# Macaron block on eight cores: the requantised hidden rows scaled in a loop of their own, ahead of the transposes

## The chip, the cores and the metric

One Trainium2 chip, 8 cores. Each core runs the same program on one of the eight batch rows of the input (4096 tokens of 1024 features), with its own copy of the weights, and no core talks to another. The metric is the device time in microseconds (us) of the slowest core.

## The reference, cut to what matters

```
x = x + 0.5 * ffn(layernorm(x))
x = x + attn(layernorm(x))
x = x + 0.5 * ffn(layernorm(x))

def ffn(x, w_gate, w_up, w_down):        # 1024 -> 4096 -> 1024
    gate = silu(bitlinear(x, w_gate))
    up   = bitlinear(x, w_up)
    return bitlinear(gate * up, w_down)
def bitlinear(x, w):                     # ternary weights, 8-bit activations
    return act_quant(x) @ weight_quant(w).T
def act_quant(x):
    scale = 127.0 / clip(max(abs(x), over the row), 1e-5)
    return clip(round(x * scale), -128, 127) / scale
```

The attention is a gated linear recurrence (four 1024x1024 products and cumulative sums over the tokens) and isn't touched by the change. What matters here is the third `bitlinear` of `ffn`: its input `gate * up` has 4096 columns a token, its scale needs the maximum over all 4096 of them, and only then can it be rounded and multiplied.

## The kernel before, in words

The program has no scheduler: every engine's instructions stand in the order in which the Python code emits them, and every dependence is a wait on one of four counting semaphores, `cT` (TensorE), `cS` (ScalarE), `cV` (VectorE), `cG` (GpSimd), or on a DMA's.

A core works through 8 chunks of 512 tokens (`NCH`), each as 4 token tiles of 128 (`TT`, index `tt`). A chunk is FFN, attention, FFN, so `emit_ffn_rest` stands 16 times in the program. The weights are turned into ternary bf16 tiles once, at the start, written to scratch in HBM (`sc_g`, `sc_u`, `sc_d`) and loaded again in every FFN.

`emit_ffn_rest` has three stages:

1. Gate and up (lines 545 to 579): 512 matmuls of 128x512. ScalarE's `Silu` (L530) and VectorE's product (L533) put the float32 hidden values into `hbuf[:, tt, :]`, and L539 takes the partial maxima.
2. Requantise and transpose (lines 585 to 610), called the block below. For each `tt`: VectorE makes the scale in five tiny operations (L586, L589, L593, L594, L599); ScalarE scales and rounds the 4096 columns in place in one activation (L602: `x * s2v + MAGIC`); TensorE transposes them, 32 pieces of 128x128 in float32, and the results go as bf16 to `hq`. The transposes are emitted by `transpose_quads` (line 373), which takes four groups ("quads") of eight pieces. Quad 0 to 3 use PSUM columns 0, 1024, 2048 and 3072, that is all eight banks. Quads 0 and 2 are evacuated by VectorE (L394), quads 1 and 3 by ScalarE (L402). TensorE's first wait in each quad is for the counts `savedV` and `savedS`, which are the numbers of VectorE and ScalarE operations emitted so far when `transpose_quads` was called.
3. Down (lines 613 to 648): 16 loads of `sc_d` (L621, issued by ScalarE's queue, two ahead, the first two once all transposes are done) and 256 matmuls (L640) into all eight banks.

Between 2 and 3, in the second FFN of a chunk except the last, `pre_next` does the layer norm, quantisation (L479) and transposes of the next chunk's input. VectorE begins it with L327.

So in the block ScalarE's queue reads: scale tile 0, evacuate two quads, scale tile 1, evacuate two quads, and so on. L602 of tile `tt+1` stands behind the evacuation of quad 3 of tile `tt`, and all transposes of `tt+1` wait for it.

Of the kernel before, what the change touches and what calls it, by code (L numbers as in the profile page):

```python
# [39 lines left out]
def build_nc(L=4096, T=512):  # L40
    NCH = L // T
    TT = T // 128
# [108 lines left out]
    cV = Sem(st, nc, "cV")  # L151
    cS = Sem(st, nc, "cS")
# [3 lines left out]
    V, S, TE, SY, G = nc.vector, nc.scalar, nc.tensor, nc.sync, nc.gpsimd  # L156
# [213 lines left out]
        cV.inc(V.tensor_scalar(out=Bq, in0=Bq, scalar1=-1.0, scalar2=MAGIC,  # L370
                               op0=ALU.mult, op1=ALU.add))

    def transpose_quads(quads, evac="copy", eng="alt"):
        savedV = [cV.n] * 4
        savedS = [cS.n] * 4
        for qi, (srcs, dst) in enumerate(quads):
            b = qi % 4
            TE.wait_ge(cV.h, savedV[b])
            TE.wait_ge(cS.h, savedS[b])
            for j, s_ in enumerate(srcs[:-1]):  # L380
                TE.transpose(out=PB[:, b * 1024 + j * 128:  # L381
                                    b * 1024 + (j + 1) * 128],
                             in_=s_, identity=ident[:, :])
            cT.inc(TE.transpose(  # L384
                out=PB[:, b * 1024 + (len(srcs) - 1) * 128:
                       b * 1024 + len(srcs) * 128],
                in_=srcs[-1], identity=ident[:, :]))
            pt = PB[:, b * 1024:b * 1024 + len(srcs) * 128]
            if eng == "V" or (eng == "alt" and qi % 2 == 0):
                cT.wait(V)  # L390
                if evac == "copy":
                    cV.inc(V.tensor_copy(out=dst, in_=pt))
                else:
                    cV.inc(V.tensor_scalar(out=dst, in0=pt, scalar1=MAGIC,  # L394
                                           scalar2=None, op0=ALU.subtract))
                savedV[b] = cV.n
            else:
                cT.wait(S)
                if evac == "copy":
                    cS.inc(S.copy(out=dst, in_=pt))  # L400
                else:
                    cS.inc(S.add(out=dst, in_=pt, add=nmagic_ap))  # L402
                savedS[b] = cS.n
# [34 lines left out]
    def emit_ffn_pre(c, xb, first_of_chunk, p, skip01=False):  # L438
# [39 lines left out]
        for tt in range(TT):  # L478
# [3 lines left out]
        cS.inc(sl_)  # L482
        cS.wait(TE)
        transpose_quads(
            [([qstage[:, tt * 1024 + ic * 128:tt * 1024 + (ic + 1) * 128]
               for ic in range(DC)],
              aq[:, tt, :, :]) for tt in range(TT)], evac="submagic")

    def emit_ffn_rest(c, xb, p, pre_next=None, attn_next=None):
# [91 lines left out]
        if c == 0:  # L581
            for s_, n_ in tern_done["d"]:
                s_.wait(V, n_)
                s_.wait(S, n_)
        for tt in range(TT):
            cV.inc(V.reduce_max(out=hmax[:, tt:tt + 1],  # L586
                                in_=hpart[:, tt * 8:tt * 8 + 8], axis=AXX))
            cV.wait(V)
            cV.inc(V.tensor_scalar(out=hmax[:, tt:tt + 1],  # L589
                                   in0=hmax[:, tt:tt + 1], scalar1=EPS_Q,  # L590
                                   scalar2=None, op0=ALU.max))
            cV.wait(V)
            V.reciprocal(out=t1[:, tt:tt + 1], in_=hmax[:, tt:tt + 1])  # L593
            cV.inc(V.tensor_scalar(out=cdv[:, tt:tt + 1],  # L594
                                   in0=hmax[:, tt:tt + 1],
                                   scalar1=cmb[:, 2:3], scalar2=None,
                                   op0=ALU.mult))
            cV.wait(V)
            cV.inc(V.tensor_scalar(out=s2v[:, tt:tt + 1], in0=t1[:, tt:tt + 1],  # L599
                                   scalar1=127.0, scalar2=None, op0=ALU.mult))  # L600
            cV.wait(S)
            cS.inc(S.activation(out=hbuf[:, tt, :], in_=hbuf[:, tt, :],  # L602
                                func=AF.Identity, scale=s2v[:, tt:tt + 1],
                                bias=magic_ap))
            cS.wait(TE)
            transpose_quads(
                [([hbuf[:, tt, ic * 128:(ic + 1) * 128]
                   for ic in range(q * 8, q * 8 + 8)],
                  hq[:, tt, q * 8:q * 8 + 8, :]) for q in range(4)],
                evac="submagic")  # L610
        if pre_next is not None:
            pre_next()
        dn_arena_cT = [cT.n, cT.n]
# [62 lines left out]
    def emit_attn(c, xb, pre01_done=False):  # L676
# [57 lines left out]
        def emit_half_mms(th):  # L734
            tt0 = th * 2
            transpose_quads(
                [([xstage(tt)[:, dc, :] for dc in range(DC)],
                  xn2T[:, :, 1 + tt * 128:1 + (tt + 1) * 128])
                 for tt in (tt0, tt0 + 1)])
            transpose_quads(  # L740
                [([xb[:, tt, dc * 128:(dc + 1) * 128] for dc in range(DC)],
                  VT[:, :, tt * 128:(tt + 1) * 128])
                 for tt in (tt0, tt0 + 1)])
            if th == 0:
                cV.wait(V)
                V.tensor_copy(out=xn2T[:, :, 0], in_=xnc)
                V.tensor_copy(out=QB[:, :, 0], in_=qc)
                cV.inc(V.tensor_copy(out=OAR[:, :, 0], in_=oarc))
            cV.wait(TE)
            cS.wait(TE)  # L750
            proj(wk1t, KB, 0, AF.Exp, b_k1, 1.0, 1, th)
            proj(wq1t, QB, 1, AF.Sigmoid, b_q1, 1.0, 1, th)
            proj(wk2t, K2B, 0, AF.Sigmoid, b_k2s, K2SCALE, 0, th)
            half_cS[th] = cS.n
            half_cV[th] = cV.n
# [315 lines left out]
    for c in range(NCH):  # L1071
        xb = xsb[c % 2]
        if c + 1 < NCH:
            if c >= 1:
                dO.wait(SY, 16 * c)
            dX[(c + 1) % 2].inc(SY.dma_start(
                out=xsb[(c + 1) % 2][:, :, :],
                in_=x_hbm.ap()[(c + 1) * T:(c + 2) * T, :]
                .rearrange("(a p) d -> p a d", p=128)), 16)
        emit_ffn_rest(c, xb, c % 2,  # L1080
                      attn_next=(lambda: attn_pre_tts(xb, (0, 1))))
        emit_attn(c, xb, pre01_done=True)
        emit_ffn_pre(c, xb, False, c % 2, skip01=True)
        pn = None
        if c + 1 < NCH:
            pn = (lambda cc: (lambda: emit_ffn_pre(cc, xsb[cc % 2], True,
                                                   cc % 2)))(c + 1)
        emit_ffn_rest(c, xb, c % 2, pre_next=pn)
        cV.wait(SY)
        cS.wait(SY)  # L1090
        dO.inc(SY.dma_start(
            out=y_hbm.ap()[c * T:(c + 1) * T, :].rearrange("(a p) d -> p a d",
                                                           p=128),
            in_=xb[:, :, :]), 16)
# [29 lines left out]
```

## Time and profile before

| | us |
|---|---|
| median of 2 runs | 6687.78 |
| the 2 runs | 6647.06 and 6728.49 |
| profiled execution, its own time | 6668.78 |
| span of its slowest core, 2 | 6667.7 |
| span of its fastest core, 7 | 6551.9 |
| granted TensorE clock, cores 0 to 7 | 0.797 to 0.813 of full |

Everything below is read on core 2. The span is the time from its first to its last instruction; 1.1 us of the profiled execution's own time lie outside it. A granted clock of 0.50 is TensorE's lower level, 1.2 GHz, and 1.00 its upper, 2.4 GHz. "Idle before" an instruction is the time in which its engine did nothing just before it, followed by the instruction that released it.

### The profile page before, as it was taken

The numbers are of one execution on the slowest core, as the hardware profiler recorded it, in microseconds if no ns is written. First come the engines' busy times: TensorE is split into PE (matmuls) and PEld (weight loads), VectorE is DVE, ScalarE is ACT, GpSimd is POOL, SyncE is SP. The second block draws the span as 40 slices with busy tenths as digits, with TensorE's granted clock in tenths as the row PEclk, the third lists the DMA queues.
The fourth block names the chain that finished last, engine by engine and source line by source line (L and its number), as shares of the span: only waits on it lengthen the run. The fifth ranks groups of instructions, "written<-read, shape, count | busy, mean of one in ns | idle before, by whom it ended". The sixth has DMA issues, their size and how long they took to land.

```text
span 6667.7 us, 52991 instructions; the slowest of 8 cores (6551.9 to 6667.7 us)
## 1 busy us (share of the span) xinstructions
PE 4048.2 (61%) x19026; PEld 2144.2 (32%) x19026; DVE 2274.5 (34%) x3475; ACT 1317.9 (20%) x1600; POOL 478.7 (7%) x505
## 2 busy tenths in 40 slices
PE   0017737875568647576377746686376763687466
PEld 0004413343233323344133332334233441333323
DVE  3433163123432243231631235232532316421442
ACT  2212112122121221121121221212121211201211
POOL 0000120002100020001200020000200012000200
PEclk6558768886789868798688978898698886898778
DMA  7983622425314343235224253143333262242522
GB/s 236 305 265 87 116 50 76 138 88 84 82 62 153 75 72 107 78 105 120 50 77 139 87 89 88 62 142 88 64 101 101 88 116 51 74 134 81 95 82 88
DMA packets 229199, 699.74 MB, mean 105 GB/s; under 512 B 22096, under 2 KB 22096, under 8 KB 224848
## 3 DMA queue, kind: packets, MB, share of 16 engines
q10 hardware_dynamic: 110592, 402.70, 19.6%
q0 software_dynamic: 76576, 159.41, 13.3%
q1 hardware_dynamic: 41776, 134.24, 6.4%
q8 instruction: 159, 2.61, 0.2%
q14 instruction: 96, 0.79, 0.0%
HBM read 788.55 MB, written 41.94 MB: 125 GB/s over the span
## 4 chain that ended last, share of the span: by engine, by line
PE 45%; DVE 20%; DMA 17%; ACT 10%; issue 6%; POOL 1%; DVEq 0%; ACTq 0%; SPq 0%; POOLq 0%
PE PB L563 11%; PE PB L568 11%; PE PB L640 9%; DMA sarena<-sc_d 8%; PE PB L381 7%; PE PB L710 5%; ACT pool L602 4%; DMA sarena<-sc_u 3%; DVE pool L533 2%; DMA pool<-wdt 2%; DMA pool<-wut 1%; DMA pool<-wgt 1%; DMA poolb<-wq1t 1%; ACT pool L530 1%; ACT pool L726 1%
## 5 line engine op out<-in xcount | busy, mean ns | idle before, releaser
L563 PE MATMUL PB<-sarena,poolb 128*128 128x512 bf16 x4096 | 1600.8, 391 | 322.3 <-DMA sarena<-sc_u 121.2
L568 PE MATMUL PB<-sarena,poolb 128*128 128x512 bf16 x4096 | 1599.4, 390 | 0.0
L381 PE MATMUL PB<-ident,pool 128*128 128x128 f32 x2464 | 504.3, 371 | 969.6 <-ACT pool L602 420.4
L640 PE MATMUL PB<-sarena,poolb 128*128 128x512 bf16 x4096 | 967.3, 396 | 183.2 <-DMA sarena<-sc_d 182.1
L533 DVE SCALAR_TENSOR_TENSOR pool<-PB,smal,pool 128x512 f32<-128x512 f32 x512 | 381.7, 746 | 1348.0 <-ACT pool L530 1347.4
L381 PEld LDWEIGHTS PB<-ident,pool 128*128 128x128 f32 x2464 | 441.3, 201 | 998.1 <-issue 998.1
L563 PEld LDWEIGHTS PB<-sarena,poolb 128*128 128x128 bf16 x4096 | 409.5, 100 | 900.1 <-issue 491.9
L640 PEld LDWEIGHTS PB<-sarena,poolb 128*128 128x128 bf16 x4096 | 401.6, 101 | 744.7 <-issue 373.2
L530 ACT ACTIVATE pool<-PB,smal 128x512 f32<-128x512 f32 x512 | 326.8, 684 | 1447.5 <-PE PB L568 1406.7
L568 PEld LDWEIGHTS PB<-sarena,poolb 128*128 128x128 bf16 x4096 | 409.2, 100 | 486.7 <-issue 77.3
L710 PE MATMUL PB<-poolb 128*128 128x256 bf16 x3072 | 408.1, 300 | 164.4 <-ACT pool L726 125.0
L653 DVE SCALAR_TENSOR_TENSOR xsb<-PB,smal,xsb 128x512 f32<-128x512 f32 x64 | 43.6, 744 | 1145.1 <-PE PB L640 1145.1
L394 DVE TENSOR_SCALAR poolb<-PB 128x1024 bf16<-128x1024 f32 x160 | 195.9, 1225 | 650.4 <-PE PB L384 650.4
L710 PEld LDWEIGHTS PB<-poolb 128*128 128x128 bf16 x3072 | 323.7, 107 | 249.2 <-issue 182.2
L539 DVE TENSOR_REDUCE smal<-pool 128x1 f32<-128x512 f32 x512 | 351.0, 686 | 54.3 <-DVE pool L533 1.9
L986 PE MATMUL PB<-poolb 128*128 128x512 bf16 x512 | 202.5, 574 | 264.4 <-DMA poolb<-wpt 152.0
L690 POOL DMA_DIRECT2D poolb<-wk1t x64 | 45.8, 719 | 4336.5 <-PE PB L640 4245.7
L402 ACT ACTIVATE poolb<-PB,smal 128x1024 bf16<-128x1024 f32 x160 | 178.1, 1113 | 407.9 <-PE PB L384 407.9
L602 ACT ACTIVATE pool<-pool,smal 128x4096 f32<-128x4096 f32 x64 | 243.1, 3799 | 73.2 <-DVE smal L599 73.1
L973 PE MATMUL PB<-bprow,onesrb 1*128 1x512 bf16 x64 | 29.8, 616 | 352.1 <-DVE poolb L897 352.1
L726 ACT ACTIVATE pool<-PB,bsb 128x256 f32<-128x256 f32 x384 | 145.2, 489 | 286.9 <-PE PB L710 286.7
L530 ACT ACT_TABLE_LOAD x16 | 20.5, 1283 | 916.9 <-PE PB L568 916.9
(132 smaller groups left out, 2595.2 us busy)
## 6 DMA issues: line engine op xcount, KB each, us to landing
sarena<-sc_g ACTq DMA_DIRECT2D x256, 512.0 KB, 4.3
sarena<-sc_u ACTq DMA_DIRECT2D x256, 512.0 KB, 5.4
sarena<-sc_d ACTq DMA_DIRECT2D x256, 512.0 KB, 4.0
pool<-wgt SPq DMA_DIRECT2D x32, 1024.0 KB, 10.8
pool<-wut SPq DMA_DIRECT2D x32, 1024.0 KB, 12.2
pool<-wdt SPq DMA_DIRECT2D x32, 1024.0 KB, 12.0
poolb<-wk1t POOLq DMA_DIRECT2D x64, 512.0 KB, 7.9
poolb<-wq1t POOLq DMA_DIRECT2D x64, 512.0 KB, 7.6
```

What stands on the lines that cost most here:

```text
L381: TE.transpose(out=PB[:, b * 1024 + j * 128: b * 1024 + (j + 1) * 128], in_=s_, identity=ident[:, :])
L394: cV.inc(V.tensor_scalar(out=dst, in0=pt, scalar1=MAGIC, scalar2=None, op0=ALU.subtract))
L530: cS.inc(S.activation(out=sl, in_=pb[ttg * 4 + (tt % 2)][:, :], func=AF.Silu, scale=cg[:, tt:tt + 1]))
L533: cV.inc(V.scalar_tensor_tensor(out=hbuf[:, tt, ob_ * 512:(ob_ + 1) * 512], in0=pb[ttg * 4 + 2 + (tt % 2)][:, :], scalar=cu[:, tt:tt + 1], ...
L539: cV.inc(V.reduce_max(out=hpart[:, tt * 8 + ob_:tt * 8 + ob_ + 1], in_=hbuf[:, tt, ob_ * 512:(ob_ + 1) * 512], axis=AXX, apply_absolute_va ...
L563: TE.matmul(out=pb[ttg * 4 + (tt % 2)][:, :], lhsT=aq[:, tt, ic, :], rhs=gsl[:, bsel * 2048 + ic4 * 512: bsel * 2048 + (ic4 + 1) * 512], s ...
L568: tl_ = TE.matmul(out=pb[ttg * 4 + 2 + (tt % 2)][:, :], lhsT=aq[:, tt, ic, :], rhs=usl[:, bsel * 2048 + ic4 * 512: bsel * 2048 + (ic4 + 1) ...
L602: cS.inc(S.activation(out=hbuf[:, tt, :], in_=hbuf[:, tt, :], func=AF.Identity, scale=s2v[:, tt:tt + 1], bias=magic_ap))
L640: tl_ = TE.matmul(out=pb[tt * 2 + obk][:, :], lhsT=hq[:, tt, ic, :], rhs=dsl[:, bsel * 2048 + ic2 * 1024 + obk * 512: bsel * 2048 + ic2 * ...
L710: tl_ = TE.matmul(out=pb[et][:, 0:HT], lhsT=aw_tile(dc, et), rhs=xn2T[:, dc, rhs_off + th * HT: rhs_off + th * HT + HT], start=(dc == 0), ...
L726: sl2 = S.activation(out=out_fm[:, et, out_off + th * HT: out_off + th * HT + HT], in_=pb[eh * 4 + ei][:, 0:HT], func=func, bias=bias_ap[: ...
L986: tl_ = TE.matmul(out=pb[th * 4 + (tt % 2) * 2 + eb][:, :], lhsT=OB_[:, dc, tt * 128:(tt + 1) * 128], rhs=aw_tile(dc, 0)[:, 0:0 + 512] if ...
```

## The change

The loop over `tt` in the block becomes two loops. The first emits, for all four tiles, the five VectorE operations and ScalarE's activation, and notes ScalarE's count after each. The second lets TensorE wait for the noted count of its tile and calls `transpose_quads`. For tile 0 the counts that the quads wait for are those taken before the first loop (`saved=hq_saved`), so that tile 0 doesn't wait for the other tiles' activations; for tiles 1 to 3 they are the counts at the call, as before.

```
-    def transpose_quads(quads, evac="copy", eng="alt"):
-        savedV = [cV.n] * 4
-        savedS = [cS.n] * 4
+    def transpose_quads(quads, evac="copy", eng="alt", saved=None):
+        v0, s0 = saved if saved is not None else (cV.n, cS.n)
+        savedV = [v0] * 4
+        savedS = [s0] * 4
...
+        hq_saved = (cV.n, cS.n)
+        p1_cS = []
         for tt in range(TT):
...
             cS.inc(S.activation(out=hbuf[:, tt, :], in_=hbuf[:, tt, :],
                                 func=AF.Identity, scale=s2v[:, tt:tt + 1],
                                 bias=magic_ap))
-            cS.wait(TE)
+            p1_cS.append(cS.n)
+        for tt in range(TT):
+            TE.wait_ge(cS.h, p1_cS[tt])
             transpose_quads(
                 [([hbuf[:, tt, ic * 128:(ic + 1) * 128]
                    for ic in range(q * 8, q * 8 + 8)],
                   hq[:, tt, q * 8:q * 8 + 8, :]) for q in range(4)],
-                evac="submagic")
+                evac="submagic", saved=hq_saved)
+            hq_saved = None
```

ScalarE's order in one block before (L530 is the last `Silu` of the gate and up stage, L602 the scaling, L402 the evacuations, L621 the loads of the down stage):

```order
L530 ACTIVATE pool<-PB,smal 128x512 x4
L602 ACTIVATE pool<-pool,smal 128x4096
L402 ACTIVATE poolb<-PB,smal 128x1024 x2
L602 ACTIVATE pool<-pool,smal 128x4096
L402 ACTIVATE poolb<-PB,smal 128x1024 x2
L602 ACTIVATE pool<-pool,smal 128x4096
L402 ACTIVATE poolb<-PB,smal 128x1024 x2
L602 ACTIVATE pool<-pool,smal 128x4096
L402 ACTIVATE poolb<-PB,smal 128x1024 x2
L621 DMA sarena<-sc_d 128x2048 x16
```

The same place after the change, where the lines are numbered anew (L531, L605, L403, L627 are the four of above):

```order
L531 ACTIVATE pool<-PB,smal 128x512 x4
L605 ACTIVATE pool<-pool,smal 128x4096 x4
L403 ACTIVATE poolb<-PB,smal 128x1024 x8
L627 DMA sarena<-sc_d 128x2048 x16
L420 ACTIVATE smal<-smal 128x2
```

Three of the four scalings have moved ahead of the first evacuation; all eight evacuations stand in a row behind the fourth.

VectorE's order in the block before, from the end of tile 0's five small operations (L599 is the last of the five, L394 the evacuation):

```order
L599 TENSOR_SCALAR smal<-smal 128x1
L394 TENSOR_SCALAR poolb<-PB 128x1024 x2
L586 TENSOR_REDUCE smal<-smal 128x1
L589 TENSOR_SCALAR smal<-smal 128x1
L593 RECIPROCAL smal<-smal 128x1
L594 TENSOR_SCALAR smal<-smal 128x1
L599 TENSOR_SCALAR smal<-smal 128x1
L394 TENSOR_SCALAR poolb<-PB 128x1024 x2
```

After the change, the end of the four sets of five (L589, L592, L596, L597 and L602 are now the five, L395 the evacuation, L659 the residual sum after the down stage):

```order
L602 TENSOR_SCALAR smal<-smal 128x1
L589 TENSOR_REDUCE smal<-smal 128x1
L592 TENSOR_SCALAR smal<-smal 128x1
L596 RECIPROCAL smal<-smal 128x1
L597 TENSOR_SCALAR smal<-smal 128x1
L602 TENSOR_SCALAR smal<-smal 128x1
L395 TENSOR_SCALAR poolb<-PB 128x1024 x8
L659 SCALAR_TENSOR_TENSOR xsb<-PB,smal,xsb 128x512 x4
```

All twenty small operations now stand ahead of the eight evacuations. TensorE's own order is the same as before; only what its transposes wait for differs.

## Rows read from the trace of the kernel before

**Rows 1.** The page: the span, and the chain that ended last, by line.

```profile
span 6667.7 us, 52991 instructions; the slowest of 8 cores (6551.9 to 6667.7 us)
...
PE PB L563 11%; PE PB L568 11%; PE PB L640 9%; DMA sarena<-sc_d 8%; PE PB L381 7%; PE PB L710 5%; ACT pool L602 4%; DMA sarena<-sc_u 3%; DVE pool L533 2%; DMA pool<-wdt 2%; DMA pool<-wut 1%; DMA pool<-wgt 1%; DMA poolb<-wq1t 1%; ACT pool L530 1%; ACT pool L726 1%
```

**Rows 2.** Groups by line: busy us, mean ns | idle before, releasers.

```profile
L381 PE MATMUL PB<-ident,pool 128*128 128x128 f32 x2464 | 504.3, 371 | 969.6 <-ACT pool L602 420.4 <-ACT pool L479 360.7 <-DVE xsb L665 125.0
...
L602 ACT ACTIVATE pool<-pool,smal 128x4096 f32<-128x4096 f32 x64 | 243.1, 3799 | 73.2 <-DVE smal L599 73.1
```

**Rows 3.** Timeline of ScalarE in one block: start, duration, instruction, idle before.

```profile
1885.70 1.26 ACT L530 ACTIVATE pool<-PB,smal 128x512 f32<-128x512 f32 x2 [2.19 <-PE PB L568]
1890.73 3.80 ACT L602 ACTIVATE pool<-pool,smal 128x4096 f32<-128x4096 f32 x1 [3.77 <-DVE smal L599]
...
1901.08 1.11 ACT L402 ACTIVATE poolb<-PB,smal 128x1024 bf16<-128x1024 f32 x1 [1.33 <-PE PB L384]
1902.51 3.80 ACT L602 ACTIVATE pool<-pool,smal 128x4096 f32<-128x4096 f32 x1 [0.31 <-DVE smal L599]
...
1912.11 1.11 ACT L402 ACTIVATE poolb<-PB,smal 128x1024 bf16<-128x1024 f32 x1 [0.63 <-PE PB L384]
1913.53 3.80 ACT L602 ACTIVATE pool<-pool,smal 128x4096 f32<-128x4096 f32 x1 [0.31 <-DVE smal L599]
...
1935.50 1.11 ACT L402 ACTIVATE poolb<-PB,smal 128x1024 bf16<-128x1024 f32 x1 [1.05 <-PE PB L384]
```

**Rows 4.** The same timeline: start and end of the first and the sixteenth block.

```profile
605.78 3.80 ACT L602 ACTIVATE pool<-pool,smal 128x4096 f32<-128x4096 f32 x1 [4.05 <-DVE smal L599]
...
649.37 1.11 ACT L402 ACTIVATE poolb<-PB,smal 128x1024 bf16<-128x1024 f32 x1 [0.63 <-PE PB L384]
...
6541.37 3.80 ACT L602 ACTIVATE pool<-pool,smal 128x4096 f32<-128x4096 f32 x1 [3.78 <-DVE smal L599]
...
6585.20 1.11 ACT L402 ACTIVATE poolb<-PB,smal 128x1024 bf16<-128x1024 f32 x1 [0.63 <-PE PB L384]
```

**Rows 5.** Timeline of TensorE in the block of rows 3: the transposes' first seven of a quad.

```profile
1894.90 1.73 PE L381 MATMUL PB<-ident,pool 128*128 128x128 f32 x7 [9.35 <-ACT pool L602]
...
1896.63 1.70 PE L381 MATMUL PB<-ident,pool 128*128 128x128 f32 x7
...
1910.10 0.93 PE L381 MATMUL PB<-ident,pool 128*128 128x128 f32 x7
...
1910.97 0.93 PE L381 MATMUL PB<-ident,pool 128*128 128x128 f32 x7
```

**Rows 6.** Stretches: us, busy of PE, PEld, DVE, ACT, POOL (count); clock, DMA share, GB/s.

```profile
1894.90:1898.10 3.20, 3.20 (x15) 3.20 (x16) 1.15 (x1) 0.00 (x0) 0.00 (x0) 0.50 0.00 0
1910.00:1912.00 2.00, 2.00 (x18) 1.77 (x16) 0.76 (x1) 1.11 (x1) 0.00 (x0) 0.98 0.00 0
3861.00:3862.60 1.60, 1.60 (x16) 1.45 (x14) 0.68 (x1) 0.00 (x0) 0.00 (x0) 1.00 0.02 5
3864.50:3866.50 2.00, 2.00 (x19) 1.76 (x19) 2.00 (x3) 0.00 (x0) 0.00 (x0) 1.00 0.00 0
2558.70:2559.70 1.00, 1.00 (x3) 0.31 (x3) 0.90 (x2) 0.44 (x1) 0.00 (x0) 0.50 0.17 41
2010.00:2030.00 20.00, 20.00 (x78) 8.10 (x77) 0.00 (x0) 0.00 (x0) 0.00 (x0) 0.81 0.39 128
2130.00:2140.00 10.00, 9.39 (x44) 4.24 (x45) 3.14 (x5) 1.38 (x2) 0.00 (x0) 1.00 0.46 139
```

**Rows 7.** Timeline of TensorE: first matmul after a short pause, in two places.

```profile
3864.42 1.80 PE L710 MATMUL PB<-poolb 128*128 128x256 bf16 x15 [1.73 <-ACT pool L400]
...
2558.61 0.59 PE L563 MATMUL PB<-sarena,poolb 128*128 128x512 bf16 x1 [2.03 <-DVE smal L539]
```

**Rows 8.** Timeline of VectorE: first and last of tile 1's five small operations.

```profile
1901.36 0.15 DVE L586 TENSOR_REDUCE smal<-smal 128x1 f32<-128x8 f32 x1
...
1902.26 0.15 DVE L599 TENSOR_SCALAR smal<-smal 128x1 f32<-128x1 f32 x1
```

## Prediction

> **What bounds the kernel now.** I read the page first, its chain of waits by line. Three matmul lines of the FFN lead it, L563, L568 and L640, and behind them stand the float32 transposes (L381, 7%) and ScalarE's scaling of the hidden rows (L602, 4%) [rows 1]. A ScalarE operation can lead a TensorE chain only if TensorE stands still for it, so the groups by line came next. L602 is busy 243 us in 64 executions of 3.80 us, and TensorE idled 420.4 us before transposes that L602 released, 6.6 us each time [rows 2]. The cause is in ScalarE's timeline: L602 of a tile ends, 6.55 us later the evacuation of quad 3 starts (1901.08 against 1894.53), it lasts 1.11 us, and only 0.31 us after its end the next L602 starts [rows 3]. Scaling and transposing alternate strictly, though they touch different tiles. TensorE restarts slowly, too. After such a pause the granted clock is 0.50, the 1.2 GHz level, later in the same burst it is 0.98 [rows 6]. A quad takes 1.70 us at the lower level and 0.87 us at the upper one (1910.10 to 1910.97) [rows 5].
>
> I measure a block from the start of its first L602 to the end of its last evacuation. The block of rows 3 takes 1935.50 + 1.11 - 1890.73 = 45.9 us; the first takes 44.7 and the sixteenth 44.9 [rows 4], and the sixteen of the timeline together 725 us, 45.3 on average. Nothing else runs in a block: the loads of the down stage and VectorE's next work follow its end. What a block loses therefore comes off the span.
>
> **The change part by part.** It adds and removes no operation. I take a tile's round as the time from the end of its scaling to the end of its last evacuation. Over the 64 tiles the quad-3 evacuation starts 5.5 to 7.3 us after the scaling's end, 6.24 on average (two of them are 6.55 and 5.80 us: 1901.08 - 1894.53 and 1912.11 - 1906.31 [rows 3]), so a round is 6.24 + 1.11 = 7.35 us.
>
> Term 1, three scalings leave the path. Before, a block is 4 x 3.80 + 4 x 7.35 = 44.6 us plus three small gaps, together 45.3, so 0.24 us a gap. Scalings 2 to 4 and their gaps were 3 x (3.80 + 0.24) = 12.1 us of waiting. They now run beside tile 0's transposes: -12.1 us.
>
> Term 2, the backlog on ScalarE. Its queue is strict: the evacuation of quad 1 of tile 0 stands behind all four scalings. Two L530 of 0.68 us each took 1.26 us together [rows 3], so back to back operations overlap by 0.1 us. The scalings end at 4 x 3.80 - 0.3 = 14.9 us and the two evacuations of tile 0 at 14.9 + 2 x 1.11 - 0.1 = 17.0 us. TensorE has transposed tile 0 by about 3.80 + 6.24 = 10.0 us, and then waits, because tile 1's quads wait for all evacuations of tile 0, and all eight banks are full anyway. Without the backlog tile 0 would have ended at 3.80 + 7.35 = 11.15 us. Cost: +5.9 us. So a little under half of term 1 comes straight back.
>
> Term 3, the clock. Tile 1 starts after about 7 us without work, longer than today's pauses, so it starts at the lower level and takes a full round. From then on nothing separates two tiles but quad 3's evacuation and a handover of 0.37 us (L602 ended at 1894.53, the transpose started at 1894.90 [rows 3, 5]): TensorE stands still for about 1.6 us instead of about 5.5. After a pause of 1.73 us the clock was still 1.00, having been 1.00 before it; after one of 2.03 us in another stage it was 0.50 [rows 6, 7]. Both happen around 2 us; the timeline has 35 pauses of 1.2 to 1.9 us that began at the upper level, and none ended at the lower one. I take tiles 2 and 3 at the upper level. A quad is 0.87 us and from the start of the last quad to its evacuation 1912.11 - 1910.97 = 1.14 us [rows 3, 5], so a round is 0.37 + 3 x 0.87 + 1.14 + 1.11 = 5.23 us, 2.1 less than 7.35. Gain: -4.2 us. If one pause in eight lets the clock fall all the same, 32 x 2.1 / 8 = 8 us of the gain are lost in the kernel.
>
> Here a rule speaks against me. The row shows a granted clock of 0.98 in a stretch that held nothing but transposes [rows 6], so in this kernel transposes do lift the clock. The Trainium skill (TensorE: Matmul & The Clock Gate, Part 4: PE-mode transpose) says that the full clock doesn't engage for transposes, since they don't count as busy in the same way. By that rule every round would be cold, as in rival B; the trace contradicts it for float32 transposes.
>
> VectorE: tile 1's five small operations took from 1901.36 to 1902.41 [rows 8], so three more sets ahead of its first evacuation are 3 x 1.3 = 4 us. They end at about 4 us in the new block, and the first quad is ready at about 6 us (0.37 + 1.70 us behind the first scaling). Cost nothing; were that cover gone, at most 4 us a block. The memory of an activation of 3.80 us beside transposes is a resource that before never shows: both read `hbuf`. No row bounds a slowdown; the nearest are ScalarE's own 3.80 us and the 1.11 us evacuations beside transposes. I take zero and leave 1 us a block for either sign.
>
> The sum: 12.1 - 5.9 + 4.2 = 10.4 us a block, 34.9 us left of 45.3. Over 16 blocks 194 - 94 + 68 = 168 us, less 8 for fallen clocks: 160 us. Of the profiled execution's 6668.8 us 6509 remain. That execution lies 19 us below the median of the two runs shown, 6687.8; the same gain from there gives 6528. I take the middle, 6518.
>
> **The rivals.**
>
> A: the short pause is enough to drop the clock. Terms 1 and 2 stay, term 3 is nothing: 6.2 us a block, 100 in all, 6569 to 6588 us, between 1% and 2% faster. For it speaks the 2.03 us pause that ended at 0.50 and that tiles would repeat burst and pause [rows 7]; against it, the pauses near 1.7 us.
>
> B: the transposes never reach the upper level in tiles 1 to 3. A cold round is 0.37 + 3 x 1.70 + about 2.0 + 1.11 = 8.6 us, a block 17.0 + 25.8 = 42.8 us, 40 us gained, about 6630 to 6650. Against it: most bursts of today reach it before their end.
>
> C: the edit doesn't do what it says, because most of what L602 cost TensorE is only exchanged for waiting on ScalarE's evacuations (the backlog is longer than I think, as when the evacuations wait twice). At 3 us more a block it leaves 50 to 110 us, 6560 to 6620. The strict queue speaks for it; the durations are all measured, which speaks against.
>
> D, the slower side: a denser TensorE makes the chip hold the clock down in the long matmul stages. In one stretch of full load the mean granted clock was 0.81, 78 matmuls in 20 us, 0.256 us each; in another it was 1.00, 44 in 10 us, 0.227 each [rows 6]. The kernel has 16 x (512 + 256) = 12288 such matmuls. If 5500 more of them, 45%, ran at 0.81, the gain of 160 us would be eaten; from there the kernel is slower. Half of them, 6144, cost 178 us, which makes 6687 on the profiled execution's count, 18 us over before. Against it: a block is 45 us of light work in 400 and gets only 10 us shorter, so the load in the matmul stages hardly changes, and both levels occur today. The Trainium skill (TensorE: Matmul & The Clock Gate, Part 1) describes a limiter that takes a die to 13/16 of the clock when three of its cores run dense matmuls; the 0.81 in the row agrees with it.
>
> **How the numbers follow.** My case (160 us) 73%, A 14%, B 4%, C 6%, D 3%. The limit of 2%, about what a measurement of this kernel can tell from no change, is 134 us, 6554. My case lies 26 us beyond it, with a few tenths of a per cent of scatter between executions, so about nine tenths of it count as faster: with a sliver of C, 0.67. A, B, most of C and the rest of my case are the same: 0.30. D: 0.03. The range: at the low end 6647 (the faster run) less 178, so 6469; at the high end A from the median, 6588, and a few us for the smaller gains: 6595.
>
> **What would show it.** ScalarE's timeline should have four scalings back to back in about 15 us, then two evacuations in 2.1 us, then pairs of evacuations. TensorE should idle some 7 us before tile 1 and 1.6 us before tiles 2 and 3, and nearly all of the 420 us should be gone except the first wait of each block (about 150 us), replaced by some 115 us of idle before tile 1 that evacuations release. Granted clock: 0.50 at the start of tile 1, 1.00 in tiles 2 and 3; a block of 34.9 us. Blocks of 39 us with 0.50 at each tile's start are A, of 43 us B. Term 2 is wrong if tile 1 starts clearly before or after 17.4 us. The forecast as a whole is wrong if the blocks shorten as said and the rest of the span grows, above all if the mean granted clock of the gate, up and down stages falls (D).

## The result, and the profile after

| | before | after |
|---|---|---|
| median, us | 6656.7 (10 runs) | 6470.64 (11 runs) |
| profiled execution, us | 6668.78 | 6463.16 |
| ratio after to before | | 0.9715, 95% interval 0.9671 to 0.9758 |

The changed kernel is 2.4 to 3.3% faster. Two of the ten executions before and two of the eleven after fell into a slower state that this program shows whatever the kernel; without them the means are 6657.0 and 6467.0 us, from which the ratio in the table comes, and the medians 6653.5 and 6455.2. The two runs of the kernel before that the prediction had to go by were high: more runs brought its median from 6687.8 down to 6656.7 us.

Where the time came from can be read off the timelines of all eight cores. I cut each into the prologue up to the first gate and up load, the sixteen gate and up stages (first load to first scaling), the sixteen blocks (first scaling to the end of the last evacuation) and the rest of the span. Means over the eight cores, in us:

| | prologue | gate and up | blocks | down, attention, layer norm | sum | one block |
|---|---|---|---|---|---|---|
| before | 379.5 | 2262.3 | 726.5 | 3240.7 | 6609.1 | 45.4 |
| after | 378.9 | 2246.9 | 544.1 | 3246.7 | 6416.6 | 34.0 |

The blocks give 182.4 us, and no core's blocks differ from the mean by more than 5 us. The gate and up stages differ by -15 us and the rest by +6 us between the two executions; nothing in the change touches them.

The page of the changed kernel, answering to [rows 1]:

```profile
span 6462.0 us, 52991 instructions; the slowest of 8 cores (6355.8 to 6462.0 us)
...
PE PB L564 12%; PE PB L569 11%; PE PB L646 9%; DMA sarena<-sc_d 8%; PE PB L382 7%; PE PB L716 5%; DVE pool L534 3%; DMA sarena<-sc_u 2%; DMA poolb<-wq1t 2%; ACT pool L605 2%; DMA pool<-wdt 2%; DMA pool<-wgt 2%; DMA pool<-wut 1%; ACT pool L531 1%; DVE smal L540 1%
```

The scaling (now L605) fell from 4% to 2% of the chain, because of a block's four scalings only the first and the fourth are still on it: the chain of the block below goes through those that start at 1844.79 and 1855.87 us. The group of the transposes, and who waited for whom, both of the changed kernel (waits: engine, line, releaser: us in total, times, longest), answer to [rows 2]:

```profile
L382 PE MATMUL PB<-ident,pool 128*128 128x128 f32 x2464 | 441.4, 339 | 854.1 <-ACT pool L480 360.4 <-ACT poolb L403 154.1 <-ACT pool L605 151.1
```

```profile
PE PB L382 <- ACT poolb L403: 154.1, 48, 7.8
PE PB L382 <- ACT pool L605: 151.1, 16, 9.8
```

Of the 420.4 us of waiting for scalings 151.1 are left, sixteen waits of 9.4 us. The other 48 waits are now for evacuations, 154.1 us. The transposes themselves are also shorter, 339 instead of 371 ns in the mean, as more of them run at the upper level of the clock.

ScalarE in one block of the changed kernel, its timeline (start, duration, instruction, idle before), answering to [rows 3]:

```profile
1844.79 14.88 ACT L605 ACTIVATE pool<-pool,smal 128x4096 f32<-128x4096 f32 x4 [3.78 <-DVE smal L589]
1859.57 2.09 ACT L403 ACTIVATE poolb<-PB,smal 128x1024 bf16<-128x1024 f32 x2
1865.55 1.11 ACT L403 ACTIVATE poolb<-PB,smal 128x1024 bf16<-128x1024 f32 x1 [3.89 <-PE PB L385]
1868.10 1.11 ACT L403 ACTIVATE poolb<-PB,smal 128x1024 bf16<-128x1024 f32 x1 [1.44 <-PE PB L385]
1871.40 1.11 ACT L403 ACTIVATE poolb<-PB,smal 128x1024 bf16<-128x1024 f32 x1 [2.18 <-PE PB L385]
1873.14 1.11 ACT L403 ACTIVATE poolb<-PB,smal 128x1024 bf16<-128x1024 f32 x1 [0.63 <-PE PB L385]
1876.44 1.11 ACT L403 ACTIVATE poolb<-PB,smal 128x1024 bf16<-128x1024 f32 x1 [2.18 <-PE PB L385]
1878.18 1.11 ACT L403 ACTIVATE poolb<-PB,smal 128x1024 bf16<-128x1024 f32 x1 [0.63 <-PE PB L385]
```

Four scalings in 14.9 us, the two late evacuations without idle time before them, which is the backlog, then three pairs that wait for TensorE. (An evacuation is the operation that empties the PSUM banks of a quad.) TensorE in the same block, the first seven transposes of each tile, answering to [rows 5]:

```profile
1848.94 1.72 PE L382 MATMUL PB<-ident,pool 128*128 128x128 f32 x7 [9.35 <-ACT pool L605]
...
1861.80 1.73 PE L382 MATMUL PB<-ident,pool 128*128 128x128 f32 x7 [7.05 <-ACT poolb L403]
...
1869.36 0.95 PE L382 MATMUL PB<-ident,pool 128*128 128x128 f32 x7 [1.36 <-ACT poolb L403]
...
1874.40 0.96 PE L382 MATMUL PB<-ident,pool 128*128 128x128 f32 x7 [1.35 <-ACT poolb L403]
```

And the clock, in stretches of the same block (length, busy of PE, PEld, DVE, ACT, POOL, then clock, DMA share, GB/s), answering to [rows 6]:

```profile
1849.00:1852.00 3.00, 3.00 (x15) 3.00 (x16) 1.01 (x1) 3.00 (x1) 0.00 (x0) 0.50 0.00 0
1862.20:1865.00 2.80, 2.80 (x15) 2.80 (x14) 1.15 (x1) 0.00 (x0) 0.00 (x0) 0.50 0.00 0
1869.40:1872.80 3.40, 3.40 (x32) 3.40 (x32) 1.74 (x2) 1.11 (x1) 0.00 (x0) 1.00 0.00 0
1874.40:1877.80 3.40, 3.40 (x31) 3.40 (x32) 1.70 (x2) 1.11 (x1) 0.00 (x0) 1.00 0.00 0
```

Tiles 0 and 1 begin at the lower level, 1.2 GHz, after pauses of 9.35 and 7.05 us; tiles 2 and 3 run wholly at the upper one, 2.4 GHz, after 1.4 us, twice as many transposes in about the same time.

### The profile page after: what moved, and what is told of

Read it like the earlier page. It is cut to its first block, busy times and chain, and to the rows that moved or that the text cites. A ratio compares the mean times of both kernels' runs of the same rounds, so it can differ in the third digit from the quotient of the medians.

```text
span 6462.0 us, 52991 instructions; the slowest of 8 cores (6355.8 to 6462.0 us)
## 1 busy us (share of the span) xinstructions
PE 3958.2 (61%) x19026; PEld 2061.0 (32%) x19026; DVE 2275.3 (35%) x3475; ACT 1310.6 (20%) x1600; POOL 479.7 (7%) x505
## 4 chain that ended last, share of the span: by engine, by line
PE 45%; DVE 20%; DMA 18%; ACT 10%; issue 6%; POOL 1%; DVEq 0%; ACTq 0%; SPq 0%; POOLq 0%
PE PB L564 12%; PE PB L569 11%; PE PB L646 9%; DMA sarena<-sc_d 8%; PE PB L382 7%; PE PB L716 5%; DVE pool L534 3%; DMA sarena<-sc_u 2%; DMA poolb<-wq1t 2%; ACT pool L605 2%; DMA pool<-wdt 2%; DMA pool<-wgt 2%; DMA pool<-wut 1%; ACT pool L531 1%; DVE smal L540 1%
## 5 line engine op out<-in xcount | busy, mean ns | idle before, releaser
L382 PE MATMUL PB<-ident,pool 128*128 128x128 f32 x2464 | 441.4, 339 | 854.1 <-ACT pool L480 360.4
L382 PEld LDWEIGHTS PB<-ident,pool 128*128 128x128 f32 x2464 | 385.4, 181 | 882.7 <-issue 882.7
L531 ACT ACTIVATE pool<-PB,smal 128x512 f32<-128x512 f32 x512 | 327.2, 684 | 1446.8 <-PE PB L569 1400.1
L659 DVE SCALAR_TENSOR_TENSOR xsb<-PB,smal,xsb 128x512 f32<-128x512 f32 x64 | 43.6, 744 | 1136.4 <-PE PB L646 1136.4
L395 DVE TENSOR_SCALAR poolb<-PB 128x1024 bf16<-128x1024 f32 x160 | 195.9, 1225 | 472.8 <-PE PB L385 472.8
L605 ACT ACTIVATE pool<-pool,smal 128x4096 f32<-128x4096 f32 x64 | 238.0, 3790 | 61.5 <-DVE smal L589 57.3
L403 ACT ACTIVATE poolb<-PB,smal 128x1024 bf16<-128x1024 f32 x160 | 176.1, 1110 | 249.7 <-PE PB L385 249.7
```

The costliest lines, as they stand in the source:

```text
L382: TE.transpose(out=PB[:, b * 1024 + j * 128: b * 1024 + (j + 1) * 128], in_=s_, identity=ident[:, :])
L395: cV.inc(V.tensor_scalar(out=dst, in0=pt, scalar1=MAGIC, scalar2=None, op0=ALU.subtract))
L531: cS.inc(S.activation(out=sl, in_=pb[ttg * 4 + (tt % 2)][:, :], func=AF.Silu, scale=cg[:, tt:tt + 1]))
```

## The experiments

All are edits of the changed kernel. Each ratio is to the kernel before. The ratios of e1, e2 and e4 leave open whether the kernel is 2% faster than the one before, and most intervals overlap, so the sure reading is the length of a block, the mean over 16 blocks and 8 cores of one profiled execution. The changed kernel stands at 34.0 us.

| | edit | ratio (95% interval) | block, us | against the changed kernel | expected |
|---|---|---|---|---|---|
| e1 | tile 0 waits for all four scalings | 0.9807 (0.974 to 0.9873) | 37.4 | +3.4 | +3.1 |
| e2 | pauses before tiles 2 and 3 longer by 1.1 us | 0.986 (0.9768 to 0.9952) | 37.8 | +3.8 | +4 to +6.6 (+2.6 if the clock never falls) |
| e3 | the same by 3.5 us | 0.9974 (0.9938 to 1.0009) | 44.4 | +10.4 | +12.0 |
| e4 | backlog longer by 3.4 us | 0.9792 (0.9736 to 0.9848) | 37.6 | +3.6 | +4.0 |
| e5 | tile 0 evacuated by VectorE | 0.9661 (0.959 to 0.9732) | 32.4 | -1.6 | -6.9 |
| e6 | only one scaling ahead | 0.9594 (0.9544 to 0.9644) | 28.3 | -5.7 | -5 to -6 |
| e7 | each quad waits for its own banks | 0.9637 (0.9568 to 0.9706) | 29.2 | -4.8 | -4 to -5 |
| e8 | e5 and e7 | 0.9546 (0.9473 to 0.9619) | 23.9 | -10.1 | -10 |
| e9 | e5 without its stray wait | 0.9581 (0.9504 to 0.9657) | 27.2 | -6.8 | -6.9 |

**e1: what the separate wait counts for tile 0 are worth.**

```
-        hq_saved = (cV.n, cS.n)
+        hq_saved = None
```

Expected:

> The changed kernel, but tile 0's quads wait for all four scalings, as the counts at the call would make them. My theory (the first scaling is on the path, the other three hide behind tile 0, and the evacuations of tile 0 stand behind them all): tile 0 starts at 14.9 + 0.4 us, takes a round of about 7.05 us, and the backlog is gone since ScalarE is free by then; then three tiles at the upper level, 5.04 us each: 14.9 + 7.05 + 15.1 = 37.1 us a block, 3.1 us more than the 34.0 us of the changed kernel, 50 us in all. Rival (the overlap of scalings and tile 0 is worth its full length): tile 0 is delayed by 11.1 us, so a block grows by 11.1 us, 178 us in all.

Measured: 37.4 us a block. ScalarE's and TensorE's timelines in one block:

```profile
1811.45 14.87 ACT L605 ACTIVATE pool<-pool,smal 128x4096 f32<-128x4096 f32 x4 [3.78 <-DVE smal L589]
...
1826.47 1.73 PE L382 MATMUL PB<-ident,pool 128*128 128x128 f32 x7 [20.21 <-ACT pool L605]
...
1834.06 0.95 PE L382 MATMUL PB<-ident,pool 128*128 128x128 f32 x7 [1.36 <-ACT poolb L403]
```

Tile 0 starts 15.0 us into the block, 10.9 us later than in the changed kernel, and the block is only 3.4 us longer. The theory holds: what tile 0 does early is mostly followed by waiting for the backlog, and tile 1 is spared its start at the lower level of the clock. One more thing stands in these rows: the fourth scaling ends at 1826.32 and the transposes start 0.15 us later, not 0.37. The section on the prediction comes back to it.

**e2 and e3: the clock as a matter of the pause.** One or three activations on scratch data (1.2 us each, a little less back to back) behind the evacuations of tiles 1 and 2. They add work whose result nothing uses.

```
             hq_saved = None
+            if tt in (1, 2):
+                for _ in range(1):      # e3: range(3)
+                    cS.wait(S)
+                    cS.inc(S.activation(out=silu2, in_=silu2,
+                                        func=AF.Identity))
```

Expected:

> One extra activation of about 1.2 us on ScalarE behind the evacuations of tile 1 and again of tile 2, so that TensorE's pauses before tiles 2 and 3 grow from 1.6 to 2.9 us; nothing else changes. If the clock doesn't fall in such a pause: two pauses of 1.3 us more, 2.6 us a block, 42 us over the changed kernel. If it falls each time, each of the two rounds is a cold one, 2.0 us longer: 6.6 us a block, 106 us. My theory, from pauses around 2 us that went both ways: some fall, 4 to 6.6 us a block, 65 to 106 us.

> Three such activations in each of the two places: pauses of 5.6 us, like those of the kernel before. Theory (term 3, the clock falls in pauses of this length and costs about 2.0 us a round): 2 x (4.0 + 2.0) = 12.0 us a block, 192 us over the changed kernel, and the granted clock at the start of tiles 2 and 3 is 0.50. Rival (the rounds of tiles 2 and 3 are short for another reason than the clock): 8.0 us a block, 128 us.

Measured: 37.8 and 44.4 us. e2 lies just below the 4 to 6.6 us expected, since the dummies were shorter than planned: the pauses grew by 1.15 us each, 2.3 us a block, and the clock took the other 1.5. TensorE in a block of e2, the first seven transposes of tiles 2 and 3:

```profile
1866.97 0.95 PE L382 MATMUL PB<-ident,pool 128*128 128x128 f32 x7 [2.50 <-ACT pool L620]
...
1873.16 1.73 PE L382 MATMUL PB<-ident,pool 128*128 128x128 f32 x7 [2.50 <-ACT pool L620]
```

Two pauses of exactly 2.50 us, one block, and the first tile starts at the upper level, the second at the lower. The stretches around the second:

```profile
1870.80:1873.00 2.20, 0.00 (x0) 0.00 (x0) 0.32 (x1) 2.11 (x2) 0.00 (x0) 0.92 0.00 0
1873.20:1874.60 1.40, 1.40 (x7) 1.40 (x8) 0.00 (x0) 0.00 (x0) 0.00 (x0) 0.50 0.00 0
```

And TensorE in a block of e3:

```profile
1894.11 1.37 PE L382 MATMUL PB<-ident,pool 128*128 128x128 f32 x7 [4.81 <-ACT pool L620]
...
1895.48 1.70 PE L382 MATMUL PB<-ident,pool 128*128 128x128 f32 x7
```

I counted, over the 256 rounds of tiles 2 and 3 of all cores, those in which the granted clock stood at 0.50 for a part of the transposes: none after pauses of 1.4 us (the changed kernel), 112 after 2.5 us (e2), 256 after 4.8 us (e3). Two more rounds of the changed kernel and 13 more of e2 ran in part at a granted clock of 0.81, which isn't a fall to the lower level. One of them, on core 7 of the changed kernel, its transposes and then the stretch:

```profile
5819.34 1.11 PE L382 MATMUL PB<-ident,pool 128*128 128x128 f32 x7 [1.35 <-ACT poolb L403]
...
5819.30:5823.70 4.40, 4.36 (x32) 4.15 (x32) 2.12 (x2) 1.11 (x1) 0.00 (x0) 0.81 0.02 4
```

The average round is 5.04, 6.9 and 10.3 us, counted from the last evacuation of the tile before, so with the pause. In e3 the added pauses are 2 x 3.45 = 6.9 us a block and the block grew by 10.4, so the clock takes 3.5 us, 1.8 a round; the rival (8.0 us) had counted longer dummies than they were, and with their true length it would have said 6.9. e3 puts the pauses before tiles 2 and 3 back to 4.8 us, near the 5.6 of the kernel before, and with that what term 3 gave: a block is within 1.0 us of the kernel before, and the ratio is 1 within its interval.

**e4: the backlog.**

```
             p1_cS.append(cS.n)
+        for _ in range(3):
+            cS.wait(S)
+            cS.inc(S.activation(out=silu2, in_=silu2, func=AF.Identity))
```

Expected:

> Three extra activations of about 1.3 us each on ScalarE between the fourth scaling and the evacuations of tile 0: the backlog of term 2 is made 4.0 us longer. Theory (ScalarE's queue sets when tile 1 starts): all of it shows, 4.0 us a block, 64 us over the changed kernel, tile 1 starting at 21.2 instead of 17.2 us. Rival (TensorE's own work on tile 0 or another wait sets it, the backlog has slack): less than 2 us a block, under 32 us.

Measured: 3.6 us a block, 57 us. ScalarE in a block:

```profile
1840.16 14.88 ACT L605 ACTIVATE pool<-pool,smal 128x4096 f32<-128x4096 f32 x4 [3.77 <-DVE smal L589]
1855.12 3.35 ACT L611 ACTIVATE pool<-pool 128x1024 f32<-128x1024 f32 x3
1858.38 2.10 ACT L403 ACTIVATE poolb<-PB,smal 128x1024 bf16<-128x1024 f32 x2
```

The dummies take 3.35 us and about 0.15 us around them, less than the 4.0 planned, and the block grew by 3.6: the backlog has no slack.

**e5: the backlog taken away, first attempt.**

```
-                evac="submagic", saved=hq_saved)
+                evac="submagic", saved=hq_saved,
+                eng="V" if tt == 0 else "alt")
```

Expected:

> The changed kernel with all four quads of tile 0 evacuated by VectorE, so that no evacuation of tile 0 stands behind the scalings. Theory (term 2): tile 0 ends at about 3.8 + 6.2 + 1.3 = 11.3 us instead of 16.9, the pause before tile 1 is 1.7 us instead of 7 and the clock stays up, tile 1's evacuations by ScalarE wait for the end of the scalings at 14.9 and end at 17.0, then two rounds of 5.04: 27.1 us a block, 6.9 us less than the changed kernel, 110 us in all. Rival (backlog has slack or VectorE's four evacuations of 1.2 us in a row take its place): under 2 us a block, under 32 us.

Measured: 32.4 us, a gain of 1.6 where 6.9 were expected. TensorE's timeline of a block that starts at 1835.66 us names the reason:

```profile
1839.83 1.73 PE L382 MATMUL PB<-ident,pool 128*128 128x128 f32 x7 [9.35 <-ACT pool L605]
...
1850.69 1.73 PE L382 MATMUL PB<-ident,pool 128*128 128x128 f32 x7 [4.71 <-ACT pool L605]
...
1857.89 0.95 PE L382 MATMUL PB<-ident,pool 128*128 128x128 f32 x7 [1.35 <-ACT poolb L403]
```

Tile 1 waits for a scaling, 4.71 us, and starts 15.0 us into the block, when the fourth scaling ends, though its own ended at about 7.5. `savedS` is ScalarE's count at the call, and with all scalings emitted that count holds all four. In the changed kernel the same wait is there, hidden behind the late evacuations. I had not seen it.

**e9: the same without that wait.**

```
-            hq_saved = None
+            hq_saved = (cV.n, hq_saved[1]) if tt == 0 else None
```

Expected:

> e5 again, but tile 1's quads no longer wait for ScalarE's count at the call, which holds all four scalings; they wait for VectorE's evacuations of tile 0 and for tile 1's own scaling alone. In e5 TensorE started tile 1 at 15.0 us, released by the fourth scaling. Theory: that count was why e5 gained 1.6 us a block and not 6.9; now tile 1 starts at about 11.5 us at the upper level, its two ScalarE evacuations follow the scalings and end at 17.0, and a block is 27.1 us, 6.9 less than the changed kernel. Rival (VectorE's four evacuations of tile 0 in a row are what costs): a block stays at 32 us.

Measured: 27.2 us a block, 0.1 from the expectation. TensorE, and VectorE's last evacuation of tile 0, in a block that starts at 1807.62 us:

```profile
1811.78 1.72 PE L382 MATMUL PB<-ident,pool 128*128 128x128 f32 x7 [9.36 <-ACT pool L605]
...
1817.70 1.22 DVE L395 TENSOR_SCALAR poolb<-PB 128x1024 bf16<-128x1024 f32 x1
1819.17 0.96 PE L382 MATMUL PB<-ident,pool 128*128 128x128 f32 x7 [2.10 <-DVE poolb L395]
1824.64 0.95 PE L382 MATMUL PB<-ident,pool 128*128 128x128 f32 x7 [1.79 <-ACT poolb L403]
1829.68 0.95 PE L382 MATMUL PB<-ident,pool 128*128 128x128 f32 x7 [1.36 <-ACT poolb L403]
```

Tile 1 starts 11.55 us into the block after a pause of 2.10 us that VectorE's evacuation ends, and at the upper level.

**e6: one scaling ahead.**

```
+        p1_scale(0)
+        p1_scale(1)
...
-            hq_saved = None
+            hq_saved = (cV.n, cS.n)
+            if tt + 2 < TT:
+                p1_scale(tt + 2)
```

(`p1_scale` is the scaling of one tile; the counts are taken before the next scaling is emitted.)

Expected:

> The changed kernel, but only one scaling ahead: the scalings of tiles 2 and 3 are emitted behind the evacuations of tiles 0 and 1. Theory: no backlog at tile 0 (its quad-3 evacuation ends at about 11.2 us, tile 1 starts at 11.6 at the upper level), but the scaling of tile 2 (11.2 to 15.0) delays the evacuations of tile 1 to 17.1, and that of tile 3 (17.1 to 20.9) those of tile 2 to 23.0, then a last round of 5.04: 28 to 29 us a block, 5 to 6 us less than the changed kernel, 80 to 96 us in all. Rival (order on ScalarE does not matter, its sum of work does): no difference.

Measured: 28.3 us, as expected. ScalarE in a block:

```profile
1814.43 7.49 ACT L609 ACTIVATE pool<-pool,smal 128x4096 f32<-128x4096 f32 x2 [3.78 <-DVE smal L590]
1822.34 1.11 ACT L403 ACTIVATE poolb<-PB,smal 128x1024 bf16<-128x1024 f32 x1 [0.41 <-PE PB L385]
1824.27 1.11 ACT L403 ACTIVATE poolb<-PB,smal 128x1024 bf16<-128x1024 f32 x1 [0.82 <-PE PB L385]
1825.28 3.80 ACT L609 ACTIVATE pool<-pool,smal 128x4096 f32<-128x4096 f32 x1
1828.98 2.11 ACT L403 ACTIVATE poolb<-PB,smal 128x1024 bf16<-128x1024 f32 x2
```

The same work on ScalarE as in the changed kernel, 24 us a block, in another order; it stands idle for 4 us of a block and not for 10. Part of the pauses before tiles 2 and 3 are now 2.0 us long, and after 79 of 184 such pauses the clock fell. On core 0 a tile started at the upper level after one of them and fell to the lower 1 us later:

```profile
615.81 0.95 PE L382 MATMUL PB<-ident,pool 128*128 128x128 f32 x7 [2.02 <-ACT poolb L403]
...
615.81:616.80 0.99, 0.99 (x9) 0.99 (x10) 0.00 (x0) 0.99 (x1) 0.00 (x0) 1.00 0.00 0
616.90:620.20 3.30, 3.30 (x18) 3.30 (x17) 1.23 (x1) 3.30 (x2) 0.00 (x0) 0.50 0.00 0
```

**e7 and e8: finer waits, alone and with e5.**

```
-        v0, s0 = saved if saved is not None else (cV.n, cS.n)
-        savedV = [v0] * 4
-        savedS = [s0] * 4
+        savedV, savedS = (saved if saved is not None
+                          else ([cV.n] * 4, [cS.n] * 4))
...
-        hq_saved = (cV.n, cS.n)
+        hq_saved = ([cV.n] * 4, [cS.n] * 4)
...
-            hq_saved = None
```

The two lists live through the four calls, so a quad waits for the last evacuation of its own two banks. e8 adds the edit of e5 (in this form without the stray wait).

Expected:

> The changed kernel, but each quad waits only for the evacuation of the quad that last used its own two banks, not for all evacuations of the tile before. Theory: tile 1's quad 0 can start at once behind tile 0 (VectorE has emptied its banks), quad 1 waits for ScalarE's backlog (about 16 us), the pauses of 1.6 us before tiles 2 and 3 vanish: about 29 to 30 us a block, 4 to 5 us less than the changed kernel, 64 to 80 us in all. Rival (the pauses are hidden by something else): under 1 us a block.

> e5 and e7 together. Theory: TensorE transposes nearly without a pause once started at 4.2 us, the scalings end at 14.9 and ScalarE's six evacuations follow; about 24 us a block, 10 us less than the changed kernel, 160 us in all, ratio to the kernel before about 0.948. Rival (the two savings are the same microseconds): no more than the larger of e5 and e7.

Measured: 29.2 and 23.9 us a block. ScalarE in a block of e8:

```profile
1785.83 14.88 ACT L604 ACTIVATE pool<-pool,smal 128x4096 f32<-128x4096 f32 x4 [3.78 <-DVE smal L588]
1800.62 2.09 ACT L402 ACTIVATE poolb<-PB,smal 128x1024 bf16<-128x1024 f32 x2
...
1808.26 1.11 ACT L402 ACTIVATE poolb<-PB,smal 128x1024 bf16<-128x1024 f32 x1 [0.63 <-PE PB L384]
```

The block ends 23.5 us after its start and is now close to ScalarE's own work, 14.9 + 6 x 1.1 us. e8 is 3.8 to 5.3% faster than the kernel before; its interval lies below that of the changed kernel, as do those of e6 and e9. Its difference to these two is smaller than the intervals: that e8 is the fastest rests on the blocks alone.

## Why the prediction was wrong: the mechanism held, a term and the base were mis-sized

The forecast was 160 us less and 6518 us, in a range from 6469 to 6595. The mean behind the ratio is 6467.0 us, the median of the same executions 6455.2 and the profiled execution 6463.2: all three lie below the range, and only the median of all eleven, 6470.6, is just inside it. The direction and the three terms came true. What failed is the size of term 3 (the round of a tile once the scalings are out of the way) with the deduction for fallen clocks, and the base.

**Term 1 and term 2** hold. The late evacuations end at 1861.66, 16.9 us into the block shown (17.0 was said), and tile 1 starts at 17.0 (17.4 was said). e4 shows that ScalarE's queue sets that moment, e1 that a start of tile 0 10.9 us later costs only 3.4 us, and e9, which takes the backlog away, gains 6.8 us.

**Term 3** is the step that failed: its mechanism holds, its size does not. Tiles 2 and 3 ran at the upper level; a round is 5.04 us, not 5.23, and tile 1's is 7.0, not 7.35. The cause is the handover of 0.37 us, which I took from the start of a tile in the kernel before. Behind the late evacuations it is 1861.80 - 1861.66 = 0.14 us, and so it is before tiles 2 and 3: 0.23 less, three times a block, 11 us in all. With the first 17.0 that were 16.9, and 45.4 us for the block before over all cores instead of 45.3, this makes up the 14 us that the blocks gained beyond my 168. The deduction of 8 us for one fallen clock in eight pauses was wrong as well: none of 256 fell. e2 shows why it was not absurd: at 2.5 us nearly half do. The pause was 1.4 us, where I had worked with 1.6.

What makes the handover 0.37 or 0.14 us is how many waits still stand ahead of the transposes in TensorE's own queue. At the start of a tile there are three: for the tile's scaling, for `savedV`, for `savedS`. When the scaling releases the first of them, the other two have still to be gone through, and it takes 0.37 us; when a ScalarE evacuation releases the last, 0.14; when VectorE's evacuation releases the middle one, as in e9 before tile 1, 0.25. e1 and e5 rule out that it is a matter of what is handed over: there the fourth scaling releases the last wait (`savedS` holds all four), and the transposes start 0.14 to 0.15 us behind it, in all 128 blocks of either. By these numbers a wait that is already satisfied costs TensorE about 0.11 us here, an estimate from (0.37 - 0.14) / 2.

**The terms put at nothing** were nothing. A scaling takes 3.79 us beside transposes where it took 3.80 without them. VectorE's last small operation ends at 1847.58 us, 2.8 us into the block, and its first evacuation starts at 1850.99.

**The base.** I took the middle of 6668.8 and 6687.8 us, 6678; the mean behind the ratio is 6657.0. That is 21 of the 51 us by which the forecast was above 6467.0. The other 30 come from the gain, 190 instead of 160: 14 from term 3 and the two small shifts named with it, 8 from the deduction, and 8 that lie outside the blocks. The low end of the range had no room for both: it took 178 us, which my terms don't give, off the faster of two runs that differ by 81 us; the blocks alone gained 182. Two executions that far apart deserved a range that also reached down by their scatter.

**The expectations by sign of waits.** The 420 us of waiting for scalings became 151.1 for the first of each block, as said (150), and 154.1 for evacuations: some 6.9 us before tile 1 and 1.4 us before tiles 2 and 3, 16 x 9.6.

**The rivals.** A (the short pause drops the clock) is refuted by the rows at 1.00 and by the count of none in 256. B (the transposes never reach the upper level) is refuted as the trace before already had it, and with it, for float32 transposes in this kernel, the rule of the Trainium skill (TensorE: Matmul & The Clock Gate, Part 4: PE-mode transpose) named in the prediction: a stretch with nothing but transposes has a granted clock of 1.00. C (the saving is only exchanged for other waits) is true of 5.8 of 12.1 us, which term 2 had counted, and of no more: the late evacuations end 16.9 us into the block, where in e6, without a backlog, tile 0 is done at 11.1. D (the long matmul stages slow down) did not happen: the gate and up stages are 15 us shorter in the mean, not longer, and the mean granted clock of the slowest cores is 0.80 before and 0.81 after.

What remains open: whether the 15 us of the gate and up stages belong to the change. Between e1 and e9 that sum varied from 2244.0 to 2273.9 us with no order to it, so I take it for scatter, but no run tested it.

## What to carry to other kernels

When a producer's operations are moved ahead of a consumer's on a strict queue, price what they are moved past as well: here half of the 12 us won on the path was given back as a backlog of evacuations, and moving one scaling ahead (e6) instead of three was worth another 5.7 us a block. A wait for "all that was emitted so far" changes its meaning when code is emitted earlier; after such a move, ask of every saved count what it now includes (e5 against e9: 5 us a block). Count the waits that stand between a release and the work it frees, also those that are long satisfied. And shortening TensorE's pauses can pay twice: behind pauses of 1.4 us the transposes here went on at the clock that the work before had reached, behind 4.8 us and more all fell to the lower level.

## What the runs showed of the hardware that I had not expected

The fall of TensorE's clock is not a matter of a pause alone. After pauses of the same 2.50 us in one block of e2 one tile started at 1.00 and the next at 0.50, and over 256 such pauses 112 fell; at 1.4 us it was none in 256 and at 4.8 us 256 in 256. Pauses of about 2 us went both ways, too: 79 of 184 fell in e6, while in e9 all 13 of 1.95 us and more before tile 2 did and none of the 47 before tile 1. What tells the two apart no run shows. In e3 the seven transposes behind the pause took 1.37 us instead of 1.73, so the first few of them still ran at the upper level before the clock fell, which is why a fallen clock cost 1.8 us a round there and 2.0 us in tile 1 of the changed kernel. The handover between ScalarE and TensorE depends on how many waits TensorE's queue has still to pass: 0.37 us with two more behind the one released, 0.25 with one (behind VectorE, e9), 0.14 with none, whether a scaling or an evacuation released it.
